# Where eight stores, a store ring and two PSUM banks are waited for: one change to a hybrid transformer pass

## The reference

```python
x = x + attn_a(_layernorm(x), ...)     # 16 heads, index mask, rank-64 keys and values
x = x + ffn(_layernorm(x), ...)        # 8 experts, top 2, and a shared one
x = x + attn_b(_layernorm(x), ...)     # 16 heads of 16, ALiBi bias, causal
x = x + ffn(_layernorm(x), ...)
```

```python
dots = relu(einsum('bqhd,bkhd->bhqk', qi, ki))
index_scores = einsum('bhqk,h->bqk', dots, idx_w)
top_k_mask = index_scores >= thr
scores = einsum('bqhd,bkhd->bhqk', q_full, k_full) * scale + combined_mask
attn = softmax(scores)
out = einsum('bhqk,bkhd->bqhd', attn, v).reshape(b, s, N_HEADS * DV)
return out @ Wo
```

## Time and profile before

| | us |
|---|---|
| time, median of 3 runs | 2616.34 (2612.78 to 2616.88) |
| the profiled execution, its own time | 2627.0 |
| span of its trace | 2625.2 |
| busy in the span: TensorE / VectorE / ScalarE / GpSimd | 2290.8 / 1799.9 / 1678.5 / 722.9 |
| stage of the first attention | 1052 |
| stage of the second attention | 465 |

### The profile page before, as it was taken

How to read it: one execution, slowest core, us unless ns; L and a number is a source line. 1 busy time by engine, 2 the same in 40 slices (tenths; PEclk the granted TensorE clock), 3 DMA queues, 4 the chain that set the end, 5 groups by cost and what they waited for, 6 DMA issues and landing times. The chain is left out here.

```text
span 2625.2 us, 42102 instructions
## 1 busy us (share of the span) xinstructions
PE 2290.8 (87%) x12536; PEld 1565.0 (60%) x12536; DVE 1799.9 (69%) x4013; ACT 1678.5 (64%) x3061; POOL 722.9 (28%) x992
## 2 busy tenths in 40 slices
PE   6956595657999999999999999899589999998995
PEld 3633363346887777877887878565344544434663
DVE  4788788875777677767776777542559888863623
ACT  3889588955777777777777777423226777775232
POOL 0115411442321432143214432136230100000163
PEclk9978797878999999999999999999778999999998
DMA  1011102131000000000000000412360101000124
GB/s 50 1 41 64 65 1 75 56 128 45 22 13 9 26 22 13 9 26 22 13 9 25 21 1 1 130 45 87 108 187 15 50 2 50 2 2 4 55 87 144
DMA packets 77562, 113.17 MB, mean 43 GB/s; under 512 B 23860, under 2 KB 51860, under 8 KB 74644
## 3 DMA queue, kind: packets, MB, share of 16 engines
q1 hardware_dynamic: 66776, 89.55, 10.9%
q0 software_dynamic: 10560, 20.86, 2.6%
HBM read 67.25 MB, written 39.58 MB: 41 GB/s over the span
## 5 line engine op out<-in xcount | busy, mean ns | idle before, releaser
L1443 DVE TENSOR_TENSOR aa_pt_lo<-psum,aa_pt_hi 128x512 fp32r<-128x512 f32 x544 | 350.7, 686 | 80.7 <-ACT aa_pt_hi L1373 78.0
L1932 DVE TENSOR_REDUCE ab_part_max<-psum 128x1 f32<-128x512 f32 (+3 forms) x640 | 348.2, 604 | 68.2 <-PE psum L1774 66.2
L1373 ACT ACTIVATE aa_pt_hi<-psum 128x512 fp32r<-128x512 f32 x544 | 297.9, 598 | 114.4 <-PE psum L1303 112.3
L1430 DVE CUSTOM_DVE_ANT_0 aa_prob<-psum,bias 128x512 f32<-128x512 f32 (+2 forms) x480 | 278.5, 598 | 116.8 <-PE psum L1293 96.8
L1880 ACT ACTIVATE ab_prob<-psum 128x512 f32<-128x512 f32 (+3 forms) x640 | 289.9, 557 | 91.4 <-PE psum L1807 89.2
L1257 POOL TENSOR_TENSOR x<-aa_y_out,x 128x256 f32<-128x256 f32 x256 | 188.7, 737 | 351.8 <-ACT aa_y_out L1391 307.4
L1291 PE MATMUL psum<-ka_hi,aa_q_hi 128*128 128x512 f32 (+3 forms) x640 | 267.6, 418 | 10.9 <-POOL aa_q_lo L1225 7.3
L1303 PE MATMUL psum<-ident,aa_prob 128*128 128x128 f32 x1600 | 253.4, 274 | 6.2 <-issue 4.8
L1365 ACT ACTIVATE aa_prob<-aa_prob,aa_neg_max 128x128 f32<-128x128 f32 (+11 forms) x192 | 228.0, 1189 | 43.4 <-DVE aa_neg_max L1436 41.7
L1314 PE MATMUL psum<-aa_pt_hi,c_stack 128*128 128x512 f32 x544 | 232.4, 427 | 5.5 <-ACT aa_out_t L1380 4.3
L1293 PE MATMUL psum<-ka_hi,aa_q_lo 128*128 128x512 f32 (+3 forms) x640 | 236.2, 369 | 0.0
(11 more groups left out here) (349 smaller groups left out, 4703.5 us busy)
## 6 DMA issues: line engine op xcount, KB each, us to landing
q_rows<-ixt_q_out SPq DMA_DIRECT2D x64, 256.0 KB, 2.1
aa_q_row<-q_rows SPq DMA_DIRECT2D x64, 256.0 KB, 2.6
f_back<-done SPq DMA_DIRECT2D x16, 512.0 KB, 7.6
w<-in_w SPq DMA_DIRECT2D x6, 896.0 KB, 9.7
x<-in_hidden SPq DMA_DIRECT2D x2, 2048.0 KB, 11.3
b_q_stack<-stash_q_hi SPq DMA_DIRECT2D x12, 256.0 KB, 3.5
b_k_stack<-stash_k_hi SPq DMA_DIRECT2D x12, 256.0 KB, 4.3
ixt_wq_n<-in_Wq_nope_T SPq DMA_DIRECT2D x2, 1024.0 KB, 5.5
```

The source lines that it names most:

```text
L1373: nc.scalar.activation(pt_hi[(TB[t] + j) % RING][:], turn_bank[(TB[t] + j) % RING], ACT.Copy).then_inc(pt_hi_done, 1)
L1430: nc.vector.tensor_tensor_reduce(prob[t % 2][h][:, c * CH:c * CH + w], score_bank[(QB[t] + h * chunks[t] + c) % 2][:, 0:w], bias[:, TRI[t] ...
L1443: nc.vector.tensor_tensor(pt_lo[ring][:], turn_bank[(TB[t] + j) % RING], pt_hi[ring][:].bitcast(F32), ALU.subtract).then_inc(pt_lo_done, 1)
L1932: nc.vector.tensor_reduce(part_max[e % 2][:, at, part:part + 1], s_bank[piece % PIECES][:, 0:w], AX.X, ALU.max).then_inc(s_used, 1)
```

## The change

It has three parts.

1. The semaphores `q_stored` are allocated outside the phases, four for each half. SyncE in `index_threshold` no longer waits for the stores at its end, but for three loads from the block's beginning. The wait moves to the places that rewrite the memory: ScalarE's `keep_high` in the next `index_scores`, and ScalarE's writes of `k_hi` in `prepare_a`.
2. In `attention_a` RING is 3 and there are OUTS = 2 result banks. The planner's rule for weigh (t, 0) is keep (t − 2), and it plans the whole order anew.
3. The eight stores are issued by SyncE at the beginning of `attention_b` (line 1602 of the changed kernel), ahead of its wait for `stashed[3]`. SyncE at the end of `prepare_b` waits for two early loads instead. ScalarE waits for `staged[0]` and `stashed[0]`, `stashed[1]` before its steps in `attention_b`.

```diff
@@ -477,6 +477,8 @@
+                for stored in q_stored:
+                    act.wait_ge(stored, 2 * NT // len(q_stored) * 16)
@@ -584,7 +586,6 @@
-        q_stored = [sem(f"q_stored{n}") for n in range(OUT)]
@@ -603,8 +604,9 @@
-                for n in range(OUT):
-                    sp.wait_ge(q_stored[n], 2 * PAIRS // OUT * 16)
+                sp.wait_ge(absorb_in, 2 * 16)
+                sp.wait_ge(heads_in, KC * 16)
+                sp.wait_ge(rope_in, 3 * 16)
@@ -1096,7 +1100,7 @@
-        put(pe, ("weigh", t, j), 463, 620, ("low", t, j), *([("keep", t - 1)] if j == 0 and t else []))
+        put(pe, ("weigh", t, j), 463, 620, ("low", t, j), *([("keep", t - 2)] if j == 0 and t >= 2 else []))
@@ -1139,7 +1143,8 @@
-    RING = 4
+    RING = 3
+    OUTS = 2
@@ -1188,7 +1193,7 @@
-        score_bank, turn_bank, out_bank = bank[0:2], bank[2:2 + RING], bank[6]
+        score_bank, turn_bank, out_bank = bank[0:2], bank[2:2 + RING], bank[5:5 + OUTS]
@@ -1307,7 +1312,7 @@
-                    out, ring = out_bank, (TB[t] + j) % RING
+                    out, ring = out_bank[t % OUTS], (TB[t] + j) % RING
@@ -1319,7 +1324,7 @@
-                    pe.wait_ge(kept, g + 1 + 1)
+                    pe.wait_ge(kept, g + 1 + OUTS)
@@ -1377,7 +1382,7 @@
-                    nc.scalar.activation(out_t[:], out_bank, ACT.Copy).then_inc(kept, 1)
+                    nc.scalar.activation(out_t[:], out_bank[t % OUTS], ACT.Copy).then_inc(kept, 1)
@@ -1393,7 +1398,7 @@
-                    act.sem_inc(kept, 1)
+                    act.sem_inc(kept, OUTS)
@@ -1511,15 +1516,8 @@
-                for j, (name, m) in enumerate(JOBS):
-                    sp.wait_ge(lo_done, NCH * (j + 1))
-                    rows = slice(0, P) if m else slice(GB * DHB, P)
-                    for part, have in (("hi", hi), ("lo", lo)):
-                        sp.dma_start(stash[f"{name}_{part}"][m * P + rows.start:(m + 1) * P, :],
-                                     have[j][rows, :].bitcast(F32)).then_inc(stashed[j], 16)
-                sp.wait_ge(staged[0], STAGE * 16)
-                for early in range(2):
-                    sp.wait_ge(stashed[early], 2 * 16)
+                sp.wait_ge(same_loaded, 16)
+                sp.wait_ge(consts_in, 2 * 16)
@@ -1597,6 +1595,15 @@
+        def store(sp):
+            for j, (name, m) in enumerate(JOBS):
+                rows = slice(0, P) if m else slice(GB * DHB, P)
+                for part, have in (("hi", hi), ("lo", lo)):
+                    sp.dma_start(stash[f"{name}_{part}"][m * P + rows.start:(m + 1) * P, :],
+                                 have[j][rows, :].bitcast(F32)).then_inc(stashed[j], 16)
+
+        return store
+
@@ -1725,6 +1732,7 @@
+                store(sp)
@@ -1904,6 +1912,9 @@
+                act.wait_ge(staged[0], STAGE * 16)
+                for early in range(2):
+                    act.wait_ge(stashed[early], 2 * 16)
@@ -2444,6 +2455,7 @@
+            q_stored = [[ctx.enter_context(nc.semaphore(f"q_stored{g}{n}")) for n in range(4)] for g in range(NT // GT)]
```

More of the change, by code:

```diff
@@ L226, in _, with index_mask @@
                     turn_verdict(NCH - 1)
-def index_mask(nc, arg, x, xT, psum, bank, const, mean, rstd, bias, bias_at, q_rows, load_early):
+def index_mask(nc, arg, x, xT, psum, bank, const, mean, rstd, bias, bias_at, q_rows, q_stored, load_early):
     with Phase(nc, "ix") as phase:
@@ L372, in index_mask @@
             index_scores(nc, f"ixs{g}", g, xT, psum, w_q, b_q, q_stack, k_stack, k_lo, q_alone, relu, weight, scores, high,
-                         low)
+                         low, q_stored[g - 1] if g else [])
             if g == 0:
@@ L378, in index_mask, with index_scores @@
             index_threshold(nc, f"ixt{g}", g, arg, xT, bank, const, scores, kth, masked, junk_act, row, flag, aim, shift,
-                            places, best, pick, bad_row, unsolved, bias, free, q_rows, load_early if g else None)
-def index_scores(nc, tag, g, xT, psum, w_q, b_q, q_stack, k_stack, k_lo, q_alone, relu, weight, scores, high, low):
+                            places, best, pick, bad_row, unsolved, bias, free, q_rows, q_stored[g], load_early if g else None)
+def index_scores(nc, tag, g, xT, psum, w_q, b_q, q_stack, k_stack, k_lo, q_alone, relu, weight, scores, high, low, q_stored):
     QC = GT * P // CH
@@ L526, in index_threshold @@
 def index_threshold(nc, tag, g, arg, xT, bank, const, scores, kth, masked, junk_act, row, flag, aim, shift, places, best,
-                    pick, bad_row, unsolved, bias, free, q_rows, load_early=None):
+                    pick, bad_row, unsolved, bias, free, q_rows, q_stored, load_early=None):
     other = slice(GT // 2, GT)
@@ L536, in index_threshold @@
     PAIRS = NT
-    RING, OUT = 3, 4
+    RING, OUT = 3, len(q_stored)
     HEADS = HG
@@ L920, in _, with prepare_a @@
                     write(halve)
-def prepare_a(nc, arg, x, xT, bank, const, k_hi, k_lo, c_stack, w_out, nowhere, early, early_at, dkv_in, tables_in, uv_in):
+def prepare_a(nc, arg, x, xT, bank, const, k_hi, k_lo, c_stack, w_out, nowhere, early, early_at, dkv_in, tables_in, uv_in, q_stored):
     with Phase(nc, "pa") as phase:
@@ L1625, in same_rows, with attention_b @@
                                         same[row:row + 1, which, :]).then_inc(same_in, 16)
-def attention_b(nc, arg, x, xT, psum, bank, const, stash, q_stack, k_stack, zeroed, staged, stashed, same_in, after, halves, values, stats):
+def attention_b(nc, arg, x, xT, psum, bank, const, store, stash, q_stack, k_stack, zeroed, staged, stashed, same_in, after, halves, values, stats):
     NG = HB // GB
@@ L2461, in load_early @@
                     sp.dma_start(early["w_uv"][:, :, n, :], arg["W_uv_T"]).then_inc(uv_in, 16)
-            index_mask(nc, arg, x, xT, psum, bank, const, mean, rstd, bias, bias_at, q_rows, load_early)
+            index_mask(nc, arg, x, xT, psum, bank, const, mean, rstd, bias, bias_at, q_rows, q_stored, load_early)
             k_hi = sb("ka_hi", [P, S], F32R, a)
@@ L2468, in program @@
             nowhere = sb("nowhere", [P, D], F32, a)
-            prepare_a(nc, arg, x, xT, bank, const, k_hi, k_lo, c_stack, w_out, nowhere, early, early_at, dkv_in, tables_in, uv_in)
+            prepare_a(nc, arg, x, xT, bank, const, k_hi, k_lo, c_stack, w_out, nowhere, early, early_at, dkv_in, tables_in, uv_in, q_stored[-1])
             attention_a(nc, arg, x, xT, bank, const, k_hi, k_lo, c_stack, bias, w_out, nowhere, q_rows, stats)
@@ L2534, in program @@
                 layernorm(nc, "ln3", x, xT, bank, const["ident"], mean, rstd, stats=stats, load=load)
-                prepare_b(nc, arg, xT, bank, weights, weights_in, stash, q_stack, k_stack, zeroed, staged, stashed, same_in[0],
-                          after, halves, values)
-            attention_b(nc, arg, x, xT, psum, bank, const, stash, q_stack, k_stack, zeroed, staged, stashed, same_in, after, halves, values, stats)
+                store = prepare_b(nc, arg, xT, bank, weights, weights_in, stash, q_stack, k_stack, zeroed, staged, stashed, same_in[0],
+                                  after, halves, values)
+            attention_b(nc, arg, x, xT, psum, bank, const, store, stash, q_stack, k_stack, zeroed, staged, stashed, same_in, after, halves, values, stats)
         with ExitStack() as f:
```

## The result

The changed kernel takes 2605.45 us (median of 9 runs, 2603.06 to 2608.60) against 2615.99 us for the kernel before (9 runs, 2612.78 to 2617.15): a ratio of 0.9962, with a 95% interval of 0.9953 to 0.9971, some 10.5 us less. The forecast was 2607.9 us, range 2598 to 2622, faster. Its profiled execution has a span of 2602.2 us against 2625.2 us. Not all of those 23 us are the change's: only 9.4 lie in stages that it touches.

| us from ... to ...

A forecast was written before the change was run, and what follows sets the result against it. The prediction took TensorE to bound the first attention (busy 1021.11 of 1047 us) and the last queue to bound block borders. −2.5 − 4.3 − 1.6 = −8.4 us took 2616.3 to 2607.9 us, range 2598 to 2622.

The forecast's parts named there:

- forecast −2.5: Ends of the index blocks: 1.8 us from no longer waiting for stores, 0.7 from clearing four fewer semaphores twice.
- forecast −4.3: First attention: keep wait −3.1, score pairs −5.7, missing turn bank +2.6, end of the body +1.9 us; bounds −20 and +18.
- forecast −1.6: Second attention: TensorE starts 9.6 us earlier but waits 8 us at the first transposed score; bounds −7.8 and +0.7.
- The keep term: First attention: first weighs wait less for the keep with two result banks, −3.1 us; bounds 0 and −7.5.
- The score pairs: First attention: five fewer score steps close behind the one two before, in four groups, −5.7 us; bounds 0 and −17.0.
- The missing turn bank and the loop's end: First attention: more weighs close behind their turn, +2.6 us; one weigh fewer ahead of the body's last, +1.9.
- fewer than 60 as a sign: First attention: scores would wait behind VectorE's take fewer than 60 times.
- The row doesn't bind: Second attention, rival: the maxima's row is not late, so the whole 9.6 us stay, 2599.9 us; chance 0.11.
- The ring runs dry: First attention, rival: three turn banks run short during long exponentials, part 2 becomes +19.7, total 2632 us; chance 0.17.
- Part 2 gives nothing: First attention, rival: the waits move to the neighbours, total 2612.2 us, no change; chance 0.24.
- That the clock might stay up in the second attention: Start of second attention, variant: with about 2 us idle TensorE may stay at 2.4 GHz, shortening the lead by little.
- Carrying the offset of the profiled execution to the median: Whole kernel: the median lies 10.7 us below the profiled execution, and this difference was assumed to hold after the change.

The follow-up runs named there:

- The runs with the same order and one result bank: Kernel before with one result bank, in an order planned for a ring of three: ratio 1.0015 with four turn banks, 1.0008 with three.
- −2.6 for it alone: Kernel before with only the eight stores issued in the second attention: ratio 0.9993; `prepare_b` and second attention 513.3 us against 515.9.
- the experiment that removed it: Changed kernel with GpSimd putting the first two events' maxima ahead of its wait for the stores: ratio 0.9932 to the kernel before, 0.9925 when repeated.
- part 2 alone: Kernel before with only three turn banks, two result banks and the newly planned order: ratio 0.9982; first attention 1047.5 us against 1051.75.

## Why the prediction was right

The time, its sign and part 2 as the largest part came out as forecast, but not each term, and part 1, net, is the smallest and not part 3. That the sum comes so near (−8.4 forecast, −9.4 in the stages that the change touches, −10.5 between the medians) is in part luck.

- **Part 1** (forecast −2.5): right at the borders, −2.4. I had the waits' place right and missed what follows: the matmuls of `prepare_a` start earlier and the clock doesn't come up earlier by as much, +1.3. Net −1.1. The step that failed is that at a border "every microsecond by which the last queue ends earlier counts, unless the next stage waits for the same thing later"; the next stage also needs its clock.
- **Part 2** (forecast −4.3; stage −6.1, −4.2 for it alone): the sum is right by errors that cancel, which is luck. The keep term was put at −3.1 and measured −9.2 (11.5 to 2.3), beyond its bound of −7.5. I took the one wait of 0.78 us at tile 8 from the matmuls' list; the first weigh there starts 1.13 us behind its cadence, and those of tiles 3 and 4 some 0.45 each, in every group. The list of the weight loads has the first as "issue" and the others among the waits behind the low part. The score pairs were put at −5.7 and measured −1.8 by the table, though up to −5.6 by another count, so whether this term missed stays open: close pairs are 4 instead of 9, but the waits on the weight loads are 74 instead of 60, where I had named fewer than 60 as a sign. The missing turn bank and the loop's end were put at +4.5 and measured +7.9 (up to +10.2). The runs with the same order and one result bank say what the sum couldn't: without the second result bank and its order part 2 would have been +2.0 in the stage.
- **Part 3** (forecast −1.6; stage −1.7, −2.6 for it alone): right step by step. TensorE starts 9.8 us earlier (11.59 − 1.79; forecast 9.6), the stores are waited for until 22.3 us after the first score (1939.81 − 1917.53; forecast 21.9), the wait is 9.3 us (forecast 8). Its last issue came 12.1 us after the first, not 13.5, and the copies ahead of it were gone, as assumed. (The bound for a landing at 1947.5 is −7.6 by its own terms, not −7.8, and part 2's upper one +18.6; neither entered the forecast.)
- **The rivals.** "The row doesn't bind" fell by the wait itself and by the experiment that removed it. "The ring runs dry" fell as a whole, though a third of it was there: weighs start 7.9 us later in all. "Part 2 gives nothing" fell by part 2 alone. That the clock might stay up in the second attention did not come true either: 0.83 at 1917 to 1921 and 0.50 after.
- **Carrying the offset of the profiled execution to the median** came out, and has a likely reason, which is not shown: its experts' stages took 428.9 us, against 415.5 to 416.4 in the group of runs whose kernel before had its median near that of the first comparison (2615.0 and 2616.0).

The Trainium skill's Perfetto Trace Analysis, section Matmuls, whose advice to rotate through PSUM banks I had called of little worth here, was the better guide: with the second result bank 9.2 us of lateness went, and a ring of three without it gave nothing.

## What to carry over

When a change advances a stage, follow what else is queued in front of the stage's first need: here 9.8 us bought 1.7, and two lines of GpSimd's order bought 9 more. Price a wait of TensorE from starts against cadence, or add the matmuls' and the weight loads' lists, "issue" included; the list of the matmuls alone showed 4.3 us where 9.2 were to be had. And where a planner makes the order, a looser limit is not by itself a faster kernel: a fourth part buffer cost 4.9 us of the stage, a fourth bank under the same order 3.8.

## What the hardware did that I had not expected

- TensorE's clock fell to 0.50 (1.2 GHz) in the lead of the second attention after only 1.79 us without work, with TensorE called busy 4.00 of 4 us and VectorE 3.99. It was back only with the transposed scores (0.76 in 1966 to 1976). No run had the whole of this lead at the full clock, so what it costs stays open.
- The eight stores ran at 227 GB/s in 1921 to 1925, among the first ones of 64 partitions, and at 428 in 1933 to 1937, among those of 128, with the DMA engines fully busy in both.
- The experts' two stages take together 415.5 to 416.4 us on one chip and 425.2 to 432.4 on the two others, for one and the same code: a difference of 9 to 17 us, about as much as the whole change or more.
